# Layer 0 of a graph network with mixing and experts: mixing and summed messages in one block, and at most two record scatters under way

## What is computed

```python
xn = layernorm(x)
# graph part of layer 0: xn goes through one linear layer (h0); each edge takes the row h0[dst] times
# its weight and adds it to the total of its source node; elu of the total
gnn = elu(segment_sum(edge_weight * (xn @ W.T + b)[dst], src))
# mixing part of layer 0: linear attention with phi(x) = x + 1 or exp(x), and a feed-forward part
q, k, v = phi(xn @ Wq + bq), phi(xn @ Wk + bk), xn @ Wv + bv      # 8 heads of 32
a = q @ (k.T @ v) / (q @ k.sum(0) + 1e-6)                          # by head
mid = layernorm(xn + a @ Wo + bo) * ln1_g + ln1_b
mix = layernorm(mid + relu(mid @ W1 + b1) @ W2 + b2) * ln2_g + ln2_b
x = x + gnn + mix
```

## Time and profile before

| | us |
|---|---|
| median of 3 runs | 7021.22 (7018.96 to 7030.24) |
| profiled execution | 7018.5 |
| its span, first to last instruction | 7016.7 |
| TensorE busy, its granted clock (mean) | 4600.0 (66%), 0.758 |
| VectorE, ScalarE, GpSimd busy | 3445.3, 1006.0, 2631.8 |

### The profile page before, as it was taken

The page is one execution under the profiler, slowest core; times in us unless marked ns, Lnnn a source line. Parts: engine busy times, 40 slices in busy tenths (PEclk is TensorE's granted clock), DMA queues, the critical chain, the costliest instruction groups (busy, mean ns, idle before and its releaser), DMA issues. The chain is left out here.

```text
span 7016.7 us, 71368 instructions
## 1 busy us (share of the span) xinstructions
PE 4600.0 (66%) x17936; PEld 3173.8 (45%) x17936; DVE 3445.3 (49%) x8060; ACT 1006.0 (14%) x2236; POOL 2631.8 (38%) x2698
## 2 busy tenths in 40 slices
PE   0486755556784577748736646588759986767644
PEld 0244543334572343324335533476637764545443
DVE  6224444443004567769851255577742233566722
ACT  0121100002221000001112210000023331111111
POOL 2345556661100455537512200566500004555332
PEclk9877776667896575559858877656679998888767
DMA  4100013333111788856512210344410003222223
GB/s 141 46 2 2 2 40 92 92 92 82 37 39 43 224 254 255 249 166 197 153 64 82 78 36 0 100 114 114 94 38 0 0 0 104 71 73 72 68 91 108
DMA packets 407468, 616.64 MB, mean 88 GB/s; under 512 B 76191, under 2 KB 303918, under 8 KB 406741
## 3 DMA queue, kind: packets, MB, share of 16 engines
q0 software_dynamic: 124448, 324.61, 16.9%
q1 hardware_dynamic: 279540, 284.98, 12.9%
q10 hardware_dynamic: 3154, 3.20, 0.2%
HBM read 475.70 MB, written 137.50 MB: 87 GB/s over the span
## 5 line engine op out<-in xcount | busy, mean ns | idle before, releaser
L837 POOL DMA_INDIRECT m_rows<-support,far_at x440 | 421.7, 958 | 1133.1 <-POOLq L97 775.5
L3169 POOL DMA_INDIRECT g_sc_rows<-keyval,src_at x440 | 438.6, 997 | 520.0 <-DVE g1b_scores L3239 227.6
L3576 POOL DMA_INDIRECT g_sp_rows<-h,src_at x440 | 438.0, 996 | 464.6 <-POOLq L97 254.1
L493 POOL DMA_INDIRECT records<-record,place_at x416 | 416.2, 1001 | 408.5 <-issue 114.4
L847 PE MATMUL g_sums_bank<-g_sums_rows,g_sums_same 128*125 128x256 f32 x880 | 351.0, 536 | 292.6 <-issue 279.2
L837 POOL DMA_INDIRECT g_sums_rows<-h,far_at x440 | 416.0, 945 | 230.1 <-issue 111.1
L3624 PE MATMUL g_sp_bank<-g_sp_rows,g_sp_same 128*125 128x264 f32 x880 | 456.7, 618 | 46.0 <-issue 22.7
L3188 PE MATMUL g_sc_pair<-g1q_parts,g_sc_near 125*128 x1320 | 333.0, 384 | 170.8 <-DVE g_sc_rows L3235 112.0
L847 PEld LDWEIGHTS g_sums_bank<-g_sums_rows,g_sums_same 128*125 128x125 f32 x880 | 197.8, 255 | 445.7 <-issue 397.7
L847 PE MATMUL m_half<-m_rows,m_same 128*125 128x256 f32 x880 | 292.3, 436 | 130.5 <-issue 125.6
L879 DVE TENSOR_TENSOR g_total<-g_total,g_sums_bank 125x256 f32 x440 | 182.8, 415 | 332.9 <-issue 158.5
(11 more groups left out here) (663 smaller groups left out, 9749.0 us busy)
## 6 DMA issues: line engine op xcount, KB each, us to landing
kept<-g_sc_rows SPq DMA_DIRECT2D x440, 128.0 KB
g_sp_rows<-kept SPq DMA_DIRECT2D x440, 128.0 KB
xnT<-sorted_rows SPq DMA_DIRECT2D x80, 256.0 KB
answer_rows<-f_answer SPq DMA_DIRECT2D x64, 256.0 KB
g_sc_local_in<-local_rows SPq DMA_DIRECT2D x55, 250.0 KB
g_sp_local_in<-local_rows SPq DMA_DIRECT2D x55, 250.0 KB
answer_rows<-zero SPq DMA_DIRECT2D x1, 9856.0 KB
sorted_rows<-zero SPq DMA_DIRECT2D x1, 8192.0 KB
```

The lines of the kernel that those rows point to most:

```text
L493: nc.gpsimd.indirect_dma_start(core.records, bass.IndirectOffsetOnAxis(ap=core.place_at[:, t:t + 1], axis=0), core.record[:, t, :], None). ...
L837: nc.gpsimd.indirect_dma_start(self.rows[:, k, :], None, self.table, bass.IndirectOffsetOnAxis(ap=core.far_at[:, s:s + 1], axis=0)).then_i ...
L3169: nc.gpsimd.indirect_dma_start(rows[:, k, :], None, table, bass.IndirectOffsetOnAxis(ap=core.src_at[:, s:s + 1], axis=0)).then_inc(gathere ...
L3576: nc.gpsimd.indirect_dma_start(self.rows[:, k, :], None, self.table, bass.IndirectOffsetOnAxis(ap=core.src_at[:, s:s + 1], axis=0)).then_i ...
```

## The change

`mix0` and the stages g0_turn and g0_sums become one block, `gnn0_mix0`. GpSimd no longer follows TensorE's slots: it issues the rest of the scatters, each behind the completion of the scatter two before it (two semaphores by parity), then waits for the arranged records and gathers. SP fetches the records once all are placed; TensorE turns them, and VectorE keeps them, right before the slot q of run 6 (START). From there on the 440 steps are dealt out behind the slots by weights (q 6, read 2 each, out 9, turn 1, hidden 16, y 20 for two tiles, so about 49 steps for a round). The banks are shared more narrowly to make room for two product banks and one for the ramp. The additions of xn and of mid are now products with the identity into the same bank, ScalarE copies the banks out, `affine` is gone, midT has two buffers, and ln0 no longer stores xn (rows=False): its place holds the total.

```diff
 class RecordPlacing:
+    def count(self, k, before):
+        return 16 * len(range(k, before, len(self.placed)))
-    def place(self, pool, count):
+    def place(self, pool, count, held=False):
...
         for t in range(self.next, self.next + count):
+            k = t % len(self.placed)
+            if held:
+                pool.wait_ge(self.placed[k], self.count(k, t))
             nc.gpsimd.indirect_dma_start(core.records, bass.IndirectOffsetOnAxis(ap=core.place_at[:, t:t + 1], axis=0),
-                                         core.record[:, t, :], None).then_inc(self.placed, 16)
+                                         core.record[:, t, :], None).then_inc(self.placed[k], 16)
     def place_rest(self, pool):
-        self.place(pool, COLUMN - self.next)
-        pool.wait_ge(self.placed, 16 * COLUMN)
+        self.place(pool, COLUMN - self.next, held=True)
+    def hold(self, eng):
+        for k, sem in enumerate(self.placed):
+            eng.wait_ge(sem, self.count(k, COLUMN))
-def arrange_records(core, name):
+class Arranging:
+    def fetch(self, sp):
+        sp.dma_start(self.rows.rearrange("p c e r -> p c (e r)"),
+                     self.core.records[0:STEPS * W, :].rearrange("(c p e) r -> p c (e r)", c=4, p=CHUNK)).then_inc(self.fetched, 16)
+    def turn(self, pe):
+        pe.wait_ge(self.fetched, 16)
...
+    def keep(self, v):
+        v.wait_ge(self.turned, 3)
...
+        v.wait_ge(self.arranged, 3)
-def gathered_sums(core, name, table, total):
...
-def mix0(core, placing):
+def gnn0_mix0(core, placing):
+    WORK = {"q": 6, "read1": 2, "read0": 2, "out": 9, "turn": 1, "hidden": 16, "y": 20}
...
+        START = next(i for i, (stage, r, _) in enumerate(slots) if (stage, r) == ("q", 6))
+        whole = sum(work for _, _, work in slots[START:])
+        until, spent = [], 0
+        for i, (_, _, work) in enumerate(slots):
+            spent += work if i >= START else 0
+            until.append(int(STEPS * spent / whole + 0.5))
+        spans = [range(until[i - 1] if i else 0, until[i]) for i in range(len(slots))]
         @block.sync
...
             sp.wait_ge(mixing.loaded, mixing.nload)
+            placing.hold(sp)
+            arranging.fetch(sp)
         @block.gpsimd
         def _(pool):
-            for stage, r in slots:
...
             placing.place_rest(pool)
+            pool.wait_ge(arranging.arranged, 3)
+            sums.gather(pool)
         @block.tensor
...
+            for i, ((stage, r, _), steps) in enumerate(zip(slots, spans)):
+                if i == START:
+                    arranging.turn(pe)
+                    pe.wait_ge(arranging.arranged, 3)
...
+                        for c in range(DC):
+                            nc.tensor.matmul(there[:, c * 128:(c + 1) * 128], core.xnT[:, c, columns(first + j)], core.ident[:], start=False, stop=False)
...
+                        for c in range(DC):
+                            nc.tensor.matmul(there[:, c * 128:(c + 1) * 128], midT[:, r % 2, c, j * P:(j + 1) * P], core.ident[:], start=False, stop=False)
...
+                for s in steps:
+                    sums.multiply(pe, s)
         @block.scalar
...
+                    nc.scalar.activation(orow[:, 0:m, :], rowbank[0:P, 0:m * D].rearrange("p (j d) -> p j d", d=D), ACT.Copy).then_inc(o_kept, 1)
...
+                    nc.scalar.activation(yrow[:, 0:m, :], rowbank[0:P, 0:m * D].rearrange("p (j d) -> p j d", d=D), ACT.Copy).then_inc(y_kept, 1)
         @block.vector
-            def affine(r):
...
+                if i == START:
+                    arranging.keep(v)
+                    sums.begin(v)
+                for s in steps:
+                    sums.add(v, s)
...
 def front(core):
-        x_in, placed = ph.sem("x_in"), ph.sem("placed")
+        x_in, placed = ph.sem("x_in"), [ph.sem(f"placed{k}") for k in range(2)]
-        layer_norm(core, "ln0", core.x, core.xn, core.xnT, ready=x_in, placing=placing)
+        layer_norm(core, "ln0", core.x, None, core.xnT, rows=False, ready=x_in, placing=placing)
-        mix0(core, placing)
+        gnn0_mix0(core, placing)
```

More of the change, by code:

```diff
@@ L879, in add, with gnn0 @@
         nc.vector.tensor_tensor(there, there, self.halves[s % len(self.halves)].unsqueeze(1), ALU.add).then_inc(self.added, 1)
-def gathered_sums(core, name, table, total):
+def gnn0(core):
     nc = core.nc
[L886 to L898, removed]
+    total = core.xn
+    with Phase(nc, "g0_fin") as inner:
+        low = inner.sb("low", [P, NT, D])
+        low_ready, grown, chain_sem = inner.sem("low_ready"), inner.sem("grown"), inner.sem("chain")
+        block = inner.block()
@@ L900, in _ @@
         @block.vector
         def _(v):
[L902 to L930, removed]
@@ new lines, in _ @@
+            chain = Chain(v, chain_sem)
+            nc.vector.tensor_scalar(low[:], total[:], 0.0, None, ALU.min).then_inc(low_ready, 1)
+            chain.link(nc.vector.scalar_tensor_tensor(core.x[:], total[:], 0.0, core.x[:], ALU.max, ALU.add))
+            v.wait_ge(grown, 1)
+            chain.link(nc.vector.scalar_tensor_tensor(core.x[:], low[:], -1.0, core.x[:], ALU.add, ALU.add))
+        @block.scalar
+        def _(act):
+            act.wait_ge(low_ready, 1)
+            nc.scalar.activation(low[:], low[:], ACT.Exp).then_inc(grown, 1)
@@ L2087, in mix0 @@
     HC = 8
+    WORK = {"q": 6, "read1": 2, "read0": 2, "out": 9, "turn": 1, "hidden": 16, "y": 20}
     with Phase(nc, "m0") as ph:
-        mixing = Mixing(core, 1.0, 1e-6, bias=True)
+        sums, mixing = Sums(core, "m0", core.h0, core.xn), Mixing(core, 1.0, 1e-6, bias=True)
         kv = [ph.ps(f"kv{k}") for k in range(2)]
         ctx = [ph.ps(f"ctx{k}") for k in range(2)]
-        nd, obank, ybank, tbank = ph.ps("nd"), ph.ps("o"), ph.ps("y"), ph.ps("t")
+        nd = ph.ps("nd")
+        halves, ramp = [ph.ps(f"half{k}") for k in range(2)], ph.ps("ramp")
         def pair(bank):
             return bank[:, 0:4 * P].rearrange("p (c n) -> p c n", c=2)
-        hbank, qbank, turnbank = [pair(bank) for bank in kv], pair(ctx[0]), pair(tbank)
-        mixing.place(ph, {"kv": kv, "ctx": ctx, "q": qbank, "nd": nd, "o": obank})
+        hbank, qbank, rowbank = [pair(bank) for bank in kv], pair(ctx[0]), ctx[1]
+        sums.place(ph, [half[0:P, 0:D] for half in halves], ramp[:, 0:P])
+        arranging = Arranging(core, ph, sums.rows[0:CHUNK].rearrange("p k d -> p (k d)")[:, 0:4 * W * RECORD].rearrange("p (c e r) -> p c e r", c=4, r=RECORD), halves + [ramp])
+        mixing.place(ph, {"kv": kv, "ctx": ctx, "q": qbank, "nd": nd, "o": rowbank})
         W1, W2 = ph.sb("W1", [128, DC, HC * 128]), ph.sb("W2", [128, HC, D])
@@ L2285, in _ @@
                 elif stage == "out":
-                    first, m = RUNS[r]
-                    v.wait_ge(mixing.out_made, r + 1)
-                    if r:
-                        v.wait_ge(normed, r)
-                    nc.vector.tensor_tensor(orow[:, 0:m, :], obank[0:P, 0:m * D].rearrange("p (j d) -> p j d", d=D), core.xn[:, first:first + m, :], ALU.add).then_inc(o_kept, 1)
+                    m = RUNS[r][1]
                     v.wait_ge(o_kept, r + 1)
@@ L2294, in _ @@
                         normalise(r)
-                elif stage == "turn":
-                    affine(r)
                 elif stage == "hidden":
```

126 lines of the change are left out of this document (64 added, 62 removed).

## The result

The changed kernel takes 7187.11 us (median of 4 runs, 7168.96 to 7192.58) where the kernel before takes 7025.35 (4 runs, 7018.96 to 7030.24): a ratio of 1.0226, 95% interval 1.0206 to 1.0247. It is slower by 162 us, 242 us from the forecast and on the other side. The profiled execution took 7192.58 us, 174 more than that of before.

A forecast was written before the change was run, and what follows sets the result against it. No engine was full in the mixing block, and the sums, a pipe of gather, product and add, had to wait for all records. Begin -115 and stretch +42 took 7018.5 to 6945.5, said as 6945 us; range 6855 to 7040.

The forecast's parts named there:

- part 2: Start of the sums: first gather at 873.7 instead of 989.0, 115 us earlier; waiting at q6 costs nothing.
- q6 reached later than the records: Sign of being wrong in the mixing block: TensorE and VectorE reach that slot only after all records lie.
- over 40%: Slowing of the early mixing that a q6 reached later than the records would mean.
- part 3: Merged stretch, first gather to last add: 374 mixing + 292 steps + 20 identity products = 686 us, replacing 644.
- part 1: Scatters with two under way: one each 1.64 us, between 1.57 and 1.70, from bounds on the landing time.
- Rival 3: Scatters: the hold never binds, period 1.26 us, first gather at 742.6, 205 us less: 6814; chance 0.05.
- rival 1: Merged stretch: in-order TensorE and VectorE wait for each other with two product banks; slower, above 7035, e.g. 7078; chance 0.13.
- Rival 2: Merged stretch: gathers alone set it, 644 us as before, only the earlier begin counts: 6903; chance 0.20.
- The sum: Whole kernel: begin -115 us and stretch +42 us make -73, from 7018.5 to 6945.5.

The follow-up runs named there:

- e1_one: The changed kernel with one scatter under way instead of two: 6874.56 us, where the kernel before takes 6625.48 on the same chip.
- at 6628: The changed kernel, unaltered, on a chip where the kernel before takes 6628.02 us: 6485.55 us, ratio 0.9779.
- e8_before_dense: The kernel before with its mixing block's 344 scatters issued in one run, not behind TensorE's slots: 6618.80 us beside 6628.02 for the kernel before.
- e3_before_dense: The kernel before with its mixing block's 344 scatters issued in one run, not behind TensorE's slots: 6626.73 us beside 6625.48 for the kernel before.
- groups 7 and 9: The changed kernel with scatters paced up to TensorE's wait and 12 or 8 gather places instead of 24: 7056.11 beside 6985.19 and 7059.58 beside 7022.82 us before.
- e9_before_dense: The kernel before with its mixing block's 344 scatters issued in one run, not behind TensorE's slots: 7384.29 us beside 7020.30 for the kernel before.

## Why the prediction was wrong

**The step that failed** is in part 2: "TensorE and VectorE reach q6 at about 601 - 6.5 in the old pacing ... so both idle some 280 us ... That costs nothing". It took over the time that the early mixing needed beside scatters paced by TensorE and used it beside scatters in one run. On the given chip q6 came at 972.7. The records were fetched at 760.75, so that with part 2's own 11.8 us the first gather could have stood at 773; the late q6 cost 207 us, scatters that were faster than forecast gave 101 of them back by luck, and the begin is 105 us later than I said. The text had named its sign among those of being wrong ("q6 reached later than the records") but built no rival on it and gave it neither price nor chance. It should have, since moving 344 scatters from 645 us of pacing into one run is the largest thing that the change does. Its "over 40%" was off, too: from m0's start at 296 instead of from zero, reaching q6 as late as 862 instead of 594 is 90% slower; measured, it took 677 us from m0's start instead of some 298. The second failed term is part 3's stretch, 133 us longer than its 686, below. 105 + 133 and the 9 us of the rest are the 247 us by which the profiled execution misses 6945.5; the median misses by 242.

**The scatter period** (part 1): forecast 1.64, bounds 1.57 to 1.77; measured (758.2 - 296.8)/343 = 1.35 on average, neighbours 1.26 apart; the hold makes GpSimd wait 11.1 us in all, in seven waits, six of them by 331.70, beside the loads of the weights. The landing is 2.36 us (e1_one), not 3.28: all three rows that I bounded it by were of other transfers or had a barrier in them. Rival 3's mechanism, a hold that doesn't bind, was right, at a chance of 0.05; its first gather, 742.6, stands beside 740.7 at 6628. The Trainium skill ("DMA: Bandwidth & Descriptors", "Anatomy of one DMA") counts about 2.0 us for the whole of a small GpSimd transfer. I had added the 0.96 of issuing to it; without that the estimate from the page is 2.0 + 0.24 = 2.24, and the 2.36 here is near it. The 0.8 us that the same page gives for a tiny transfer ("Latency and other measured facts") is a floor there, and no scatter here comes near it.

**The stretch** (part 3): forecast 686, measured 819 and, at 6628, 609. The step period on the given chip is 793.5/440 = 1.80 us, beyond the 1.73 from which rival 1 decides, and the time fell into rival 1's region (above 7035, chance 0.13). But rival 1's reason, two banks for the products and in-order engines, isn't enough: the same code with the same banks runs at 590.9/440 = 1.34 us a step at 6628. What failed is that both of the numbers compared, the 644 of g_sums and the 686, were taken as the code's own. The base is 560 at 6628. There the stretch grows by 49 us, close to the 42 of the forecast (20 for the identity products, 22 for what TensorE's queue has beyond the 644 of g_sums); on the given chip it grows by 175. The 126 us between the two growths are what part 3 had no term for. Rival 2, no growth at all, held on neither chip.

**The sum** at 6628 came out on the forecast side: -142 us against -73. The growth of the stretch was about right (+49 against +42), and the begin was better than forecast (-187 against -115), since the scatters were faster and q6 wasn't late. That agreement is of the difference; the forecast's absolute numbers were built on the given chip.

**What could have been read before.** The trace of before had the sign in it. The waits in its g_sums, and below them those of e8_before_dense, whose g_sums is the same code on a 6628 chip:

```profile
PE g_sums_bank L847 <- issue: 279.2, 153, 4.5
DVE g_total L879 <- remote: 107.8, 39, 4.9
```

```profile
PE g_sums_bank L847 <- DMA g_sums_rows<-h,far_at: 53.4, 104, 1.9
PE g_sums_bank L847 <- DVE g_total L879: 25.4, 41, 0.7
```

On the given chip TensorE's products wait 279 us for nothing that the profile names and VectorE for something "remote", on the other for the gather and for the bank, which is what a pipe of gather, product and add must wait for. I had read the 1.43 us a gather of the earlier trace rows as the pipe's own pace; in e8_before_dense it is 1.25. The 14.54 us of the earlier trace rows, which I put down to VectorE's division chain, are "issue" too, and the same wait is 10.9 us in e8_before_dense. And in ln0 of before, beside the first run of 20 scatters, a normalization of 0.41 us stands behind 6.70 us of idle time (230.11), and twice more behind 5.14 and 3.28; in e3_before_dense, whose ln0 is the same, none stands behind 2 us or more.

**What stays open.** That scatters in one run stretch the key tiles on a 7020 chip is shown. That the gathers do the same in the merged stretch is only argued: from the place of the extra time (where indirect DMAs run), from TensorE standing while GpSimd issues, and from the waits for "issue" and "remote"; no run spaced the gathers. Which resource is held isn't shown for either: the DMA engines are at 3% beside the scatters, what the waiting engines need was made long before, and ScalarE is kept from its first operation for 27.0 us tile after tile. Whether the two kinds are two sorts of chip or a condition that one chip can be in isn't known either; groups 7 and 9, at different levels, carried the same chip number, and the records don't say whether it was the same machine. Whether a gather pace between 1.25 us in runs and none would free TensorE in the merged stretch wasn't tried, and the early pacing with 24 places wasn't met by a 7020 chip.

## What to carry to other kernels

A long run of GpSimd's indirect DMAs need not be free cover for other engines: where the change gathers such transfers into a run, price the work beside it at a stretch where they already run back to back, and look there for waits put down to "issue" or "remote" on engines whose producers are long done. Put the run where the others wait anyway: on such a chip, pacing up to the wait and the rest in one run put the first gather 114 and 117 us ahead of that of before, against 10 in the changed kernel; on the other kind it gave up 92 us. And time the kernel before beside every variant: here one kernel was 2.3% slower on one chip and 2.2% faster on another.

## What the runs showed of the hardware

- The same kernel takes some 7020 or some 6625 us (before, 0.755 to 0.758 and 0.769 to 0.776 of the clock granted on average); about 390 of the 400 us lie in stretches that have indirect transfers in them.
- On the 7020 kind, scatters issued each 1.26 us bring ScalarE's key tiles from 3.83 to 28.00 us and the old pace is back 26 us after the last scatter; the first late tile was due 30 us into the run in e9_before_dense and 43 us in the changed kernel. Scatters each 2.36 us, or two behind each key tile, leave these tiles alone; two or three behind each later stage go with rounds of 43.6 us instead of 41.1.
- A scatter of 128 records of 16 bytes is seen landed by GpSimd 2.36 us after its start, 0.96 of it issuing; with two under way GpSimd waits 11.1 us in all over 344 of them.
